# Routing a mixture of experts batch by batch inside the attention ahead of it, in a gated cross-attention stack

## The chip, the cores and the metric

The kernel runs on one core of a Trainium2 chip. The metric is the device time of one execution in microseconds (us). Three runs of the kernel before took 2361.58, 2368.78 and 2369.87 us; the median is 2368.78 us.

## The reference, cut to what matters

Eight batches of 256 rows with 256 features pass through four layers. Each layer adds a gated attention branch and then a gated feed-forward branch. The feed-forwards of layers 1 and 2 are mixtures of experts in which every row goes to 2 of 8 experts:

```python
x = x + tanh(g_xattn[1]) * L1_xattn(layernorm(x), ctx_768, mask, ...)     # stage l1x
x = x + tanh(g_ffn[1])   * L1_ffn(layernorm(x), ...)                      # stage l1f
x = x + tanh(g_xattn[2]) * L2_xattn(layernorm(x), ctx_768, ...)           # stage l2x
x = x + tanh(g_ffn[2])   * L2_ffn(layernorm(x), ...)                      # stage l2f
...
# L1_ffn: hidden width 682
gate_logits = x @ Wg.T ; top 2 of 8 ; gating = softmax over the two logits
out = sum over e of gating[e] * ((silu(x @ W1[e].T) * (x @ W2[e].T)) @ W3[e].T)
# L2_ffn: hidden width 256, and two shared experts that every row passes
scores = softmax(xt @ gate_w.T) ; top 2 of (scores + gate_bias) ; weights = scores of the two
out = sum over e of gate_e * expert_e(xt) + (silu(xt @ sw1.T) * (xt @ sw3.T)) @ sw2.T
```

## The kernel before

All 2048 rows stay in SBUF as `x`, 16 tiles of 128 rows, two tiles a batch (T = 2, B = 8, NT = 16, NE = 8 experts). Each engine runs its own list of instructions in the order in which it was written; engines wait for one another on semaphores. TensorE (PE) multiplies, VectorE (DVE), ScalarE (ACT) and GpSimd (POOL) do the rest, SyncE (SP) issues most DMAs. The stages run in the order l0x, l0f, l1x, l1f, l2x, l2f, l3x, sim, l3f; a semaphore `phase` counts the finished ones.

**Attention.** `packing` (l1x, l3x, l3f) runs over n = -3 .. B and inside over 16 heads h. While the heads of one batch are computed, the projections of batch n + 3 and the output of batch n - 1 are interleaved with them at fixed h; batch n - 1 is added to `x` on DVE at h = 8 (L1248). The scores that DVE takes maxima of (L1167) go round three PSUM banks in l1x and two in l3x; other results use "rooms", PSUM banks handed out in turn, two in l1x and three in l3x. `wide` (l2x) runs over i, 16 heads a batch, in the same way: POOL normalises each head's probabilities (L849, L852), PE transposes them three heads later, batch n is added to `x` at i = 16(n + 1) + 7 (L1096).

**Mixture.** `mixture` first chooses for all 16 tiles at once: DVE statistics (L923, L934), POOL the power -1/2 (L734), DVE the normal rows into `r.all` (L1326), PE transposes and logits (L2329, L2319), DVE the ranks of the 8 logits of a row (L1331 to L1357), PE the counts of rows ahead for each expert (L2339), DVE the slots and the numbers of the blocks and gates (L1370 to L1412). POOL then writes every row to its two places in the DRAM table `rows_by_expert` by 32 indirect DMAs (L807). SP reads the table back, 512 rows a job (L552), and the 15 jobs of experts begin. An expert's weights are split into a high and a low part on POOL (L793, L795) before PE multiplies (L1875 to L1877); l1f holds two sets of weights (ring 2), l2f five. In l2f four jobs on the shared experts stand ahead of the 15, but they too begin after the choice. The table is cleared once, by one DMA from ACT in l0f, and l2f uses it again.

## Time and profile before

| | |
|---|---|
| runs, us | 2361.58, 2368.78, 2369.87 |
| profiled execution, us | 2362.5 |
| its span, us | 2360.8 |
| PE, DVE, ACT, POOL busy | 81%, 58%, 34%, 33% |
| l1x ends, first product of the experts of l1f | 481.9 us, 584.4 us |
| l2x ends, first product of l2f | 1471.4 us, 1526.6 us |

The busy shares are means over stages. In l1x and l2x PE is busy nearly all the time; between the end of an attention and the first product of the experts it mostly waits.

### The profile page before, as it was taken

The numbers are of one execution on the slowest core, as the hardware profiler recorded it, in microseconds if no ns is written. First come the engines' busy times: TensorE is split into PE (matmuls) and PEld (weight loads), VectorE is DVE, ScalarE is ACT, GpSimd is POOL, SyncE is SP. The second block draws the span as 40 slices with busy tenths as digits, with TensorE's granted clock in tenths as the row PEclk, the third lists the DMA queues.
The fourth block names the chain that finished last, engine by engine and source line by source line (L and its number), as shares of the span: only waits on it lengthen the run. The fifth ranks groups of instructions, "written<-read, shape, count | busy, mean of one in ns | idle before, by whom it ended". The sixth has DMA issues, their size and how long they took to land.

```text
span 2360.8 us, 33280 instructions
## 1 busy us (share of the span) xinstructions
PE 1904.9 (81%) x11976; PEld 1489.9 (63%) x11976; DVE 1368.9 (58%) x2894; ACT 803.2 (34%) x1761; POOL 779.7 (33%) x694
## 2 busy tenths in 40 slices
PE   3579699941999999959999997599957888547997
PEld 2467566541777777747877776588855555335664
DVE  2434478551554444447677775565536898456774
ACT  1122146510222222136555553113312454123554
POOL 3110111055245444337666554635532200100000
PEclk9789779655999999979999999599975797777999
DMA  4280356213233333221111102025628542015341
GB/s 131 84 286 0 51 84 86 29 76 125 90 126 119 112 112 103 83 74 45 31 31 39 27 19 76 25 99 174 192 75 111 80 63 29 1 22 69 61 75 43
DMA packets 125310, 186.26 MB, mean 79 GB/s; under 512 B 11940, under 2 KB 106212, under 8 KB 122532
## 3 DMA queue, kind: packets, MB, share of 16 engines
q1 hardware_dynamic: 96212, 136.75, 25.5%
q0 software_dynamic: 8448, 26.52, 3.7%
q10 hardware_dynamic: 20496, 20.97, 2.7%
q8 instruction: 93, 1.52, 0.3%
q14 instruction: 61, 0.50, 0.1%
HBM read 89.26 MB, written 47.19 MB: 58 GB/s over the span
## 4 chain that ended last, share of the span: by engine, by line
PE 54%; issue 14%; DVE 13%; POOL 10%; DMA 5%; ACT 3%; SPq 1%; DVEq 0%; POOLq 0%; ACTq 0%
PE bank L1875 10%; PE bank L1876 8%; PE bank L1877 8%; PE bank L2156 6%; PE bank L2188 4%; POOL ewl L795 3%; DMA ew<-in_we 3%; PE bank L2008 2%; DVE nmf L1167 2%; PE bank L2025 2%; PE bank L2051 2%; PE bank L2173 1%; PE bank L2036 1%; POOL ewh L793 1%; POOL rows_by_expert L807 1%
## 5 line engine op out<-in xcount | busy, mean ns | idle before, releaser
L1167 DVE TENSOR_REDUCE nmf<-bank 128x2 f32<-128x512 f32 x384 | 260.3, 688 | 112.0 <-PE bank L2156 108.9
L1748 ACT ACTIVATE pT<-bank 128x512 f32<-128x512 f32 x384 | 224.8, 597 | 250.7 <-PE bank L2173 248.4
L1430 DVE TENSOR_TENSOR bank<-sil,bank 128x512 f32<-128x512 f32 x136 | 94.8, 697 | 283.1 <-ACT sil L1803 282.6
L2156 PE MATMUL bank<-kpack,qpack 48*128 48x256 f32 (+1 forms) x768 | 199.8, 367 | 52.4 <-DVE nmf L1167 28.5
L1875 PE MATMUL bank<-split,ewl 128*128 128x512 f32 x514 | 211.4, 411 | 24.0 <-POOL ewl L795 16.3
L1876 PE MATMUL bank<-split,ewh 128*128 128x512 f32 (+1 forms) x578 | 228.2, 395 | 0.0
L1877 PE MATMUL bank<-split,ewh 128*128 128x512 f32 (+1 forms) x578 | 227.3, 393 | 0.0
L2156 PEld LDWEIGHTS bank<-kpack,qpack 48*128 48x128 f32 (+1 forms) x768 | 127.4, 220 | 131.9 <-DVE nmf L1167 61.8
L795 POOL TENSOR_TENSOR ewl<-ew,ewh 128x1536 fp32r<-128x1536 f32 (+1 forms) x47 | 206.0, 4384 | 3.8
L2173 PE MATMUL bank<-qpack,kpack 50*128 50x256 f32 (+1 forms) x768 | 198.7, 360 | 9.5 <-ACT pT L1748 9.4
L793 POOL CAST ewh<-ew 128x1536 fp32r<-128x1536 f32 (+1 forms) x47 | 85.2, 1814 | 321.0 <-DMA ew<-in_we 310.1
L1803 ACT ACTIVATE sil<-bank 128x512 f32<-128x512 f32 x136 | 81.3, 598 | 320.0 <-PE bank L1877 320.0
L1649 ACT ACTIVATE w<-bank,nmax 128x256 f32<-128x256 f32 x256 | 118.9, 469 | 168.0 <-DVE nmax L1050 166.7
L1875 PE MATMUL bank<-ewh,split 128*128 128x256 f32 x544 | 167.2, 307 | 6.5 <-issue 6.5
L1876 PE MATMUL bank<-ewl,split 128*128 128x256 f32 x544 | 155.7, 286 | 0.0
L1877 PE MATMUL bank<-ewh,split 128*128 128x256 f32 x544 | 155.2, 285 | 0.0
L734 POOL TENSOR_TENSOR rstd<-rstd,mhalf 128x2 f32<-128x2 f32 x40 | 28.4, 711 | 376.5 <-DVE rstd L1151 247.3
L2173 PEld LDWEIGHTS bank<-qpack,kpack 50*128 50x128 f32 (+1 forms) x768 | 124.3, 213 | 25.9 <-ACT pT L1748 20.0
L1050 DVE TENSOR_REDUCE nmax<-bank 128x2 f32<-128x512 f32 x128 | 88.1, 689 | 87.6 <-PE bank L2025 86.1
L1875 PEld LDWEIGHTS bank<-split,ewl 128*128 128x128 f32 x514 | 97.6, 190 | 62.7 <-DVE split L1433 21.0
L852 POOL TENSOR_TENSOR w<-w,esum 128x512 f32<-128x512 f32 x128 | 133.2, 1040 | 10.1
L849 POOL TENSOR_TENSOR esum<-esum,minus 128x2 f32<-128x2 f32 x128 | 89.7, 701 | 139.1 <-ACT w L1649 138.8
(432 smaller groups left out, 4623.4 us busy)
## 6 DMA issues: line engine op xcount, KB each, us to landing
ew<-in_we SPq DMA_DIRECT2D x32, 768.0 KB, 7.6
ew<-in_we SPq DMA_DIRECT2D x15, 1408.0 KB, 6.2
rows_by_expert<-zeros ACTq DMA_DIRECT2D x1, 20480.0 KB, 62.9
kpack<-khl SPq DMA_DIRECT2D x144, 128.0 KB, 4.0
qpack<-qhl SPq DMA_DIRECT2D x144, 128.0 KB
arena<-rows_by_expert SPq DMA_DIRECT2D x23, 512.0 KB, 4.2
rows_by_expert<-arena SPq DMA_DIRECT2D x38, 256.0 KB, 5.3
split<-split SPq DMA_DIRECT2D x64, 128.0 KB, 2.5
```

The costliest lines, as they stand in the source:

```text
L793: nc.gpsimd.tensor_copy(high, whole).then_inc(m["wh"], 1)
L795: nc.gpsimd.tensor_tensor(low, whole, high, ALU.subtract).then_inc(m["ws"], 1)
L852: nc.gpsimd.tensor_tensor(p3, p3, total.rearrange("p (t o) -> p t o", o=1).broadcast_to([P, T, S]), ALU.mult).then_inc(m["pn"], 1)
L1167: V.tensor_reduce(nmf[:, c, :, j, r], bank[s.banks[i % len(s.banks)]][:, :] .rearrange("p (t k) -> p t k", t=T), AXX, ALU.max, negate=True ...
L1430: tt(whole, sil[n % 2][rr, :], whole, ALU.mult).then_inc(m["prod"], 1)
L1649: ins = A(probs[i % 4][:, t * S:(t + 1) * S], bank[i % 2][:, t * S:(t + 1) * S], ACT.Exp, bias=nmax[:, h, t:t + 1], accum_out=esum[:, h, t ...
L1748: A(pT16[i % 8][:, :], bank[2 + h % 2][:, :], ACT.Exp, scale=s.qscale).then_inc(m["e"], 1)
L1875: mm(out_, al, bh, start=start, stop=False)
L1876: mm(out_, ah, bl, start=False, stop=False)
L1877: return mm(out_, ah, bh, start=False, stop=stop)
L2156: ins = mm(bank[s.banks[i % len(s.banks)]][:, t * S:(t + 1) * S], q[rows, r, t * P:(t + 1) * P], k[rows, r, :], start=True, stop=True)
L2173: ins = mm(bank[2 + h % 2][:, t * S:(t + 1) * S], k[rows, r, t * P:(t + 1) * P], q[rows, r, :], start=True, stop=True)
```

## The change

Each batch is routed by itself, in the attention that ends with it, as soon as its rows are final. Statistics, normal rows, transposes, logits, ranks, running sums, slots and the writing of the rows (4 indirect DMAs a batch) are interleaved with the heads of the next two batches. `csum` carries how many rows each expert has so far, so that no batch needs the later ones. Part of the small arithmetic moves from DVE to POOL. l1x routes all eight batches (its loop gets two more rounds, in which only routing is left), l2x routes seven and the eighth is routed in l2f, beside the shared experts. Each mixture has a table of its own; the second is cleared by ten DMAs of 2 MB from ACT in jobs 2 to 11 of l1f. l1x now uses two banks for scores and three rooms. In l1f the first set of weights is split by ACT and DVE instead of POOL; the numbers of the blocks and the gates are worked out there ahead of the first job, in l2f within job 1.

```diff
-        self.banks, self.rooms = ((0, 1), (5, 6, 7)) if self.proj else ((0, 1, 5), (6, 7))
+        self.banks, self.rooms = (0, 1), (5, 6, 7)
+        self.last = B + 3 if mask else B + 1
...
@@ POOL, l1x @@
+                    if s is L1X and 0 <= n - 2 < B:
+                        route_rank(L1F, n - 2)
+                        route_sums(L1F, n - 2)
+                    if s is L1X and 0 <= n - 1 < B:
+                        route_root(L1F, n - 1)
...
+                        route_slots(L1F, n - 2, m[f"mf{b}"], at[f"mf{b}"] + k + 1)
+                        route_scatter(L1F, n - 2)
...
+            def route_rank(s, n):
+                pool.wait_ge(rt["cmp"], s.turn * B + n + 1)
+                tt(same, same, tri[:, :, :].rearrange("p (o e) j -> p o e j", o=1).broadcast_to([P, T, NE, NE]), ALU.mult)\
+                    .then_inc(rt["choice"], 1)
+                tt(more_, more_, same, ALU.add).then_inc(rt["choice"], 1)
+                tt(more_[:, :, :, 0:4], more_[:, :, :, 0:4], more_[:, :, :, 4:8], ALU.add).then_inc(rt["choice"], 1)
...
+            def route_scatter(s, n):
+                pool.wait_ge(rt["slot"], s.turn * B + n + 1)
+                for t in range(T):
+                    for w in range(2):
+                        nc.gpsimd.indirect_dma_start(
+                            tables[s.name].rearrange("b s d -> (b s) d"),
+                            bass.IndirectOffsetOnAxis(ap=sli[s.name][:, w, n * T + t:n * T + t + 1], axis=0),
+                            routed(n, t)[:, :], None).then_inc(mo[f"sc{n % 2}"], 16)
@@ POOL, mixture @@
-                root({"asked": asked[s.name]}, 1, rstda[:, :], rstda[:, :], mhalf[:, 0:NT])
-                pool.wait_ge(g["xn"], entered(s.name, B) * T)
-                for w in range(s.ring):
+                if s.shared:
+                    route_root(s, B - 1)
+                    split_set(0)
+                    route_rank(s, B - 1)
+                    split_set(1)
+                    route_sums(s, B - 1)
+                    route_slots(s, B - 1, rt["trc"], 1)
+                    route_scatter(s, B - 1)
+                else:
+                    pool.wait_ge(m["ws"], at["ws"] + s.parts)
+                for w in range(2 if s.shared else 1, s.ring):
                     split_set(w)
@@ POOL, l2x @@
+                    if i % 16 == 8 and 0 <= i // 16 - 1 < B - 1:
+                        route_root(L2F, i // 16 - 1)
+                    if i % 16 == 4 and 0 <= i // 16 - 2 < B - 1:
+                        route_rank(L2F, i // 16 - 2)
...
+                    if i % 16 == 12 and 0 <= i // 16 - 2 < B - 1:
+                        route_scatter(L2F, i // 16 - 2)
@@ DVE, l1x @@
+                        if s is L1X and h == 8 and 0 <= n - 1 < B:
+                            if n == B:
+                                free()
+                            route_stats(L1F, n - 1, ch)
+                        if s is L1X and h == 3 and 0 <= n - 2 < B:
...
+                            route_compare(L1F, n - 2)
+                        if s is L1X and h == 8 and 0 <= n - 2 < B:
+                            route_chosen(L1F, n - 2)
+                        if s is L1X and h == 14 and 0 <= n - 2 < B:
+                            route_places(L1F, n - 2, ch, *made("tr", n - 2))
+                        if s is L1X and h == 1 and 0 <= n - 3 < B:
+                            route_cast(L1F, n - 3)
@@ DVE, mixture @@
+                    for p in range(s.parts):
+                        dve.wait_ge(rt["high"], p + 1)
+                        whole, low, high = (weights(t, s, 0, p) for t in (ew, ewl, ewh))
+                        tt(low, whole, high, ALU.subtract).then_inc(m["ws"], 1)
...
+                if not s.shared:
+                    blocks_and_gates()
+                    low_part(0)
+                    low_part(1)
@@ PE @@
+            def route_turn(s, n, to, done):
+                pe.wait_ge(rt["rows"], s.turn * B + n + 1)
+                for t in range(T):
+                    for c in range(DC):
+                        ins = tr(to[:, c * S + t * P:c * S + (t + 1) * P], routed(n, t)[:, c * P:(c + 1) * P], ident[:, :])
+                ins.then_inc(done, 1)
+            def route_ranks(s, n, to, done):
+                pe.wait_ge(rt["pick"], s.turn * B + n + 1)
+                mm(to[:, 0:(T + 1) * NE], ones[:, :], csum[:, n * T:n * T + T + 1, :].rearrange("p t e -> p (t e)"),
+                   start=True, stop=False)
+                mm(to[:, 0:T * NE], strict[:, :], lg[:, n * T:n * T + T, :].rearrange("p t e -> p (t e)"), start=False, stop=True)\
+                    .then_inc(done, 1)
@@ ACT, l1f @@
+                    if not s.shared and 2 <= k < 12:
+                        act.dma_start(tables["l2f"][4 * k - 8:4 * k - 4, :, :].rearrange("b s d -> (b s) d")
+                                      .rearrange("(p k) d -> p k d", p=P), zeros[:, 0:1, :].broadcast_to([P, 16, D]))\
+                            .then_inc(g["zero2"], 16)
```

DVE where l1x ends and l1f begins, before (`x` is the last batch's sum, `lg` and `scr` hold logits and ranks of all tiles):

```order
L1248 SCALAR_TENSOR_TENSOR x<-both,tgx,x 128x512
L1318 MEMSET idle 128x1
L923 BN_STATS bsta<-x 128x6 x2
L932 MEMSET idle 128x1
L934 BN_AGGR mva<-bsta 128x2 x16
L936 TENSOR_SCALAR rstda<-mva 128x16
L1326 TENSOR_SCALAR arena<-x,mva,rstda 128x256 x16
L1331 COPY lg<-bank 128x128
L1332 TENSOR_REDUCE gm<-lg 128x16
L1333 TENSOR_TENSOR sel<-lg,gm 128x128
L1334 MEMSET idle 128x1
L1347 TENSOR_TENSOR scr<-lg 128x1024
```

The same place of the changed kernel (`sli_l1f` are the slots of one batch, `ewl` the low part of the first set of weights):

```order
L1428 SCALAR_TENSOR_TENSOR x<-both,tgx,x 128x512
...
L1106 TENSOR_TENSOR scr<-sel 128x128
L1107 TENSOR_TENSOR scr<-sel 128x128
L1113 TENSOR_SCALAR larger<-scr 128x16
L1114 TENSOR_SCALAR lg<-scr 128x16
L1118 COPY totals<-bank 128x8
L1119 TENSOR_TENSOR scr<-bank,ebase 128x16
L1125 CAST sli_l1f<-slf 128x2x2
L1557 TENSOR_TENSOR ewl<-ew,ewh 128x2816
L1557 TENSOR_TENSOR ewl<-ew,ewh 128x1536
L1558 TENSOR_REDUCE gm<-sel 128x16
L1559 TENSOR_TENSOR sel<-sel,gm 128x128
```

The sixteen normalised tiles and the operations over all tiles are gone from here; what is left is one batch's, and two subtractions of weights.

POOL in the middle of l2x, before (a head is one `esum` and one `w` row, L779 gathers rows of the mixture before):

```order
L734 TENSOR_TENSOR rstd<-rstd,mhalf 128x2
L779 DMA w<-rows_by_expert,sli 128x256 x4
L849 TENSOR_TENSOR esum<-esum,minus 128x2
L852 TENSOR_TENSOR w<-w,esum 128x512
L849 TENSOR_TENSOR esum<-esum,minus 128x2
L852 TENSOR_TENSOR w<-w,esum 128x512
```

The same place of the changed kernel:

```order
L750 TENSOR_TENSOR rstd<-rstd,mhalf 128x2
L870 DMA w<-rows_by_expert_l1f,sli_l1f 128x256 x4
L940 TENSOR_TENSOR esum<-esum,minus 128x2
L943 TENSOR_TENSOR w<-w,esum 128x512
L815 TENSOR_TENSOR scr<-scr,tri 128x128
L818 TENSOR_TENSOR scr<-scr 128x128
L820 TENSOR_TENSOR scr<-scr 128x16x4
L822 TENSOR_TENSOR scr<-scr 128x16x2
L824 TENSOR_TENSOR scr<-scr 128x16
L940 TENSOR_TENSOR esum<-esum,minus 128x2
L943 TENSOR_TENSOR w<-w,esum 128x512
```

Five additions for the ranks stand between two heads; nine more small operations and four indirect DMAs follow further down in the same batch.

## Rows read from the trace of the kernel before

**Rows 1.** Busy time by stretch: us, PE, PEld, DVE, ACT, POOL, PEclk, DMA share, GB/s.

```profile
340.00:360.00 20.00, 18.71 (x184) 12.70 (x180) 16.70 (x38) 12.55 (x24) 2.58 (x3) 1.00 0.70 93
...
440.00:460.00 20.00, 19.02 (x117) 10.65 (x106) 8.39 (x17) 8.91 (x18) 0.00 (x0) 0.50 0.01 2
...
482.00:530.00 48.00, 21.38 (x100) 20.73 (x100) 28.30 (x67) 5.09 (x9) 30.73 (x9) 0.50 0.24 93
530.00:583.00 53.00, 2.19 (x9) 1.83 (x10) 5.80 (x24) 1.09 (x2) 31.50 (x33) 0.50 0.36 124
...
1166.00:1218.00 52.00, 49.27 (x342) 41.17 (x341) 38.77 (x66) 29.89 (x92) 34.39 (x40) 0.97 0.14 35
```

**Rows 2.** Timeline between l1x and the experts of l1f: start, us, engine, operation, idle before.

```profile
481.15 0.75 DVE L1248 SCALAR_TENSOR_TENSOR x<-both,tgx,x 128x512 f32<-128x512 f32 x1
...
530.79 1.12 POOL L807 DMA_INDIRECT rows_by_expert<-arena,sli  x1 [10.13 <-DVE idle L1383]
...
570.19 0.96 POOL L807 DMA_INDIRECT rows_by_expert<-arena,sli  x1 [0.30 <-issue]
...
578.63 1.97 PE L2356 MATMUL bank<-ident,arena 128*128 128x128 f32 x8 [52.07 <-DMA arena<-rows_by_expert]
...
584.37 0.78 PE L1875 MATMUL bank<-split,ewl 128*128 128x512 f32 x1
```

**Rows 3.** Timeline between l2x and the products of l2f.

```profile
1470.60 0.75 DVE L1096 SCALAR_TENSOR_TENSOR x<-scr,tgx,x 128x512 f32<-128x512 f32 x1
...
1526.55 0.78 PE L1875 MATMUL bank<-split,ewl 128*128 128x512 f32 x1
```

**Rows 4.** Groups of POOL instructions over the span: shape, count, busy, mean ns, idle.

```profile
L795 POOL TENSOR_TENSOR ewl<-ew,ewh 128x1536 fp32r<-128x1536 f32 x32 | 112.7, 3522 | 2.6
L795 POOL TENSOR_TENSOR ewl<-ew,ewh 128x2816 fp32r<-128x2816 f32 x15 | 93.3, 6221 | 1.2
L849 POOL TENSOR_TENSOR esum<-esum,minus 128x2 f32<-128x2 f32 x128 | 89.7, 701 | 139.1 <-ACT w L1649 138.8
...
L807 POOL DMA_INDIRECT rows_by_expert<-arena,sli x64 | 61.8, 965 | 41.2 <-DVE idle L1383 22.3 <-issue 18.9
L793 POOL CAST ewh<-ew 128x1536 fp32r<-128x1536 f32 x32 | 47.2, 1474 | 87.9 <-DMA ew<-in_we 82.5 <-DVE arena L1326 5.4
L793 POOL CAST ewh<-ew 128x2816 fp32r<-128x2816 f32 x15 | 38.1, 2538 | 233.0 <-DMA ew<-in_we 227.7 <-DVE arena L1326 5.4
```

**Rows 5.** Timeline of the choice of l1f: DVE beside POOL, and the block numbers.

```profile
508.73 6.11 POOL L795 TENSOR_TENSOR ewl<-ew,ewh 128x2816 fp32r<-128x2816 f32 x1
508.76 6.22 DVE L1333 TENSOR_TENSOR sel<-lg,gm 128x128 f32<-128x128 f32 x1
...
529.82 0.17 DVE L1387 TENSOR_SCALAR more<-upto 128x8 f32<-128x8 f32 x1
...
534.94 0.29 DVE L1412 TENSOR_REDUCE gw_l1f<-scr 128x16 f32<-128x128 f32 x1
```

**Rows 6.** Timeline of PE: four transposes in l1x, four and logits in l1f.

```profile
361.74 0.66 PE L2107 MATMUL bank<-ident,xn 128*128 128x128 f32 x4
...
493.96 1.09 PE L2329 MATMUL bank<-ident,arena 128*128 128x128 f32 x4
...
494.84 1.71 PE L2319 MATMUL bank<-wg,xt 128*128 128x8 f32 x8
```

**Rows 7.** Waits, 1114 to 1426 us: waiting line, what it waited for, total, times, longest.

```profile
PE bank L2051 <- DVE sil L1057: 10.6, 5, 2.1
```

**Rows 8.** Waits, 584 to 1000 us.

```profile
PE bank L1875 <- POOL ewl L795: 16.3, 13, 2.7
```

**Rows 9.** The page's DMA queues and issues: packets, MB, share; KB each, us to landing.

```profile
q10 hardware_dynamic: 20496, 20.97, 2.7%
...
ew<-in_we SPq DMA_DIRECT2D x15, 1408.0 KB, 6.2
rows_by_expert<-zeros ACTq DMA_DIRECT2D x1, 20480.0 KB, 62.9
```

More of the change, by code:

```diff
@@ L79, in jobs @@
             jobs.append(("x", (i + 9) // 16))
+        for what, at, back in (("tx", 11, 1), ("tl", 15, 1), ("tr", 7, 2)):
+            if i % 16 == at and 0 <= i // 16 - back < B - 1:
+                jobs.append((what, i // 16 - back))
         return jobs
@@ L471, in build @@
         asked, requests = {}, 0
-        for n, one in (("l0x", 1 + B), ("l0f", 1 + B), ("l1x", B), ("l1f", 1), ("l2x", B), ("l2f", 1), ("l3x", B),
+        for n, one in (("l0x", 1 + B), ("l0f", 1 + B), ("l1x", B), ("l2x", B), ("l3x", B),
                        ("sim", 2), ("l3f", B)):
@@ L480, in entries @@
         def entries(name, n):
-            return n + sum(B for k in n_phase if n_phase[k] < n_phase[name] and k not in packs and k != L2X.name)
+            return n + sum(B for k in n_phase if n_phase[k] < n_phase[name] and k in ("l0x", "l0f", "sim"))
         def entered(name, n):
-            return n + (n_phase[name] - 1) * B
+            return n + sum(B for k in n_phase if n_phase[k] < n_phase[name] and k not in ("l1f", "l2f"))
         @block.sync
@@ L757, in packing @@
                     gather(L2F, 2)
[L758 removed]
+                for n in range(-3, B + 2 if s is L1X else B):
                     p = n + 3
@@ L1264, in finish, with free @@
                                 ALU.mult, ALU.add))
+                def free():
+                    for b, rooms_ in enumerate(s.rooms):
+                        last = max(k for (what, n), (r, k) in s.place.items() if r == b and what[0] != "t")
+                        dve.wait_ge(m[f"mf{b}"], at[f"mf{b}"] + last + 1)
+                    V.memset(idle[:, 0:1], 0.0).then_inc(g["phase"], 1)
                 def clipped(i):
@@ L1274, in packing @@
                 normal(0)
-                for n in range(-3, B + 1):
+                if s is L1X:
+                    ch.link(V.memset(csum[:, 0, :], 0.0))
+                for n in range(-3, s.last):
                     for h in range(NH):
@@ L1294, in packing @@
                             register_maxima(n + 2)
-                        if n == B and h < B - 1 and not s.own:
+                        if n == B and h < B - 1 and s is L3X:
                             stats_of(h)
@@ L1314, in packing @@
                     finish(B - 1)
-                for b in range(2):
-                    dve.wait_ge(m[f"mf{b}"], at[f"mf{b}"] + s.used[b])
+                if s is not L1X:
+                    free()
                 s.total["dve"] = ch.k
-                V.memset(idle[:, 0:1], 0.0).then_inc(g["phase"], 1)
                 return at["dve"] + ch.k
@@ L1374, in mixture @@
-                ch.link(tt(before, before, bank[1][:, NT * NE:2 * NT * NE].rearrange("p (e t) -> p e t", e=NE), ALU.add))
-                ch.link(tt(part[2], before.rearrange("p e t -> p t e"), ebase[:, 0:1, :].broadcast_to(full), ALU.add))
-                for w in range(2):
-                    ins = tt(part[w], part[2], both[w][:, :, :], ALU.mult)
-                ch.link(ins)
-                for w in range(2):
-                    ins = V.tensor_reduce(slf[:, w, :], part[w], AXX, ALU.add)
@@ L1381, in mixture @@
-                ch.link(ins)
-                ch.link(V.tensor_copy(sli[:, :, :], slf[:, :, :]))
-                V.memset(idle[:, 0:1], 0.0).then_inc(m["sl"], 1)
-                extra, start, end, value = (more[:, k, :] for k in range(4))
-                rows_of = upto[:, :, NT - 1]
-                ch.link(ts(extra, rows_of, 512.0, None, ALU.is_gt))
-                ch.link(stt(extra, rows_of, 1024.0, extra, ALU.is_gt, ALU.add))
-                ch.link(stt(extra, rows_of, 1536.0, extra, ALU.is_gt, ALU.add))
@@ L1741, in gathered, with route_copy, route_rows @@
                     copy(oT16[:, 2 * f:2 * f + 2, :], halves(bank[4])).then_inc(m["oc"], 1)
+                def route_copy(n):
+                    if n > 0:
+                        made("tl", n - 1)
+                    from_, done = made("tx", n)
+                    copy(xt[:, :, :], halves(from_)).then_inc(done, 1)
+                def route_rows(n):
+                    act.wait_ge(rt["root"], 3 * n + 3)
+                    act.wait_ge(mo[f"sc{n % 2}"], L1F.base[f"sc{n % 2}"] + 64 * (n // 2))
+                    for t in range(T):
+                        r = n * T + t
+                        ins = A(routed(n, t)[:, :], x[:, r, :], ACT.Identity, scale=rstda[:, r:r + 1], bias=shift[:, t:t + 1])
+                    ins.then_inc(rt["rows"], 1)
                 def exponent(n, h):
@@ L1755, in packing @@
                     copy(masks[:, :, :], halves(from_[0:16, :])).then_inc(done, 1)
-                for n in range(-3, B + 1):
+                for n in range(-3, s.last):
                     for h in range(NH):
@@ L2269, in packing @@
                     ins.then_inc(done, 1)
-                for n in range(-3, B + 1):
+                for n in range(-3, s.last):
                     for h in range(NH):
```

448 lines of the change are left out of this document (297 added, 151 removed).

## The prediction

> **What bounds the kernel now.** I read the busy time by stretch first. In l1x, PE is busy 18.71 of 20 us at a granted clock of 1.00 (2.4 GHz), DVE 16.70; in l2x PE 49.27 of 52, POOL 34.39; but between 482 and 583 us PE works 23.6 of 101 us, at 0.50 (1.2 GHz) [rows 1]. The timelines give that hole its edges. From the end of the last sum of l1x (481.15 + 0.75 = 481.9) to the first product of l1f (584.37) pass 102.5 us; from the last sum of l2x (1471.35) to the first product of l2f (1526.55) pass 55.2 us [rows 2, 3]. Within the first hole, 40 us go to the 32 indirect writes, which POOL starts 1.265 us apart (570.19 - 530.79, divided by 31), and 13.2 us from the end of the last write (571.15) to the product: landing, reading back, transposing, splitting [rows 2]. The holes sum to 157.7 us. The attentions that are to take this work in have little room: PE about 6% in both, and DVE 17% in l1x.
>
> **The choice of l1f.** What can't be streamed is the last batch. I follow its chain from 481.9. Prices: DVE as at 529.82 to 535.23, some 0.2 to 0.3 us an operation [rows 5]; POOL's subtractions of 1536 and 2816 columns take 3.52 and 6.22 us, so 2.11 ns a column and 0.28 us fixed, which I extend down to 0.3 to 0.55 us for the small ones; a power on two columns takes 0.70 [rows 4]. In order: statistics 1.4; DVE marks the experts of batch 6, 0.4; POOL's sums for it and the three operations on the last batch's root, 2.2; POOL's slots of batch 6, 1.6, and DVE's cast, 0.2; the four writes of batch 6, 5.1 (the last batch's rows, transposes 1.1, logits 1.7 and comparison lie beside these [rows 6]); then the last batch: ranks 2.2, marks 0.4, sums 0.6, counts on PE 1.0, places 0.5, slots 1.6, cast 0.3, writes 5.1. Together 22.6, and about 1.0 for some fifteen handovers: the last write ends at 505.5, not 571.15.
>
> With the same 13.2 us behind it the first product would come at 518.7. But DVE must first finish the block numbers and gates, which now precede `low_part(0)`, and POOL splits the second set of weights at that very time: 2.54 + 6.22 + 1.47 + 3.52 = 13.8 us, from 505.5 to 519.3 [rows 4]. In the trace a DVE operation on two SBUF tensors that began 0.03 us behind POOL's 6.11 us subtraction took 6.22 us, where its like take 0.3 [rows 5]. So I let DVE pass one such operation for each of POOL's four, leave about 5 of its 5.4 + 1.6 us of work until after 519.3, and add the 3.0 us that low part, transposes and first product took: first product at 527.3, a gain of 57 us. Bounds: 68 if DVE isn't held and the small POOL operations take 0.3; 48 if every one takes 0.70 and DVE gets nothing done before POOL ends.
>
> **The choice of l2f.** Seven batches are routed when l2x ends, but the seventh's cast and four writes still stand before POOL's root of the eighth: 1.6 statistics, 1.0 places, 1.6 slots, 5.1 writes, 0.7 root. The eighth batch's rows then go through 0.7 rows, 1.1 transposes, 0.6 copy, 1.1 high, 0.7 low, 2.0 transposes, 1.0 logits: the first product comes 17 us after l2x ends, not 55.2, a gain of 38. Part is given back. Sum over the first shared job: PE needs the second set before its third tile and also waits for the running sums, which POOL reaches only after ranks (from 22 us) and a split of 5.0: 7 us of stall. Then in job 1 DVE's 7 us of numbers meet POOL's splits of sets 2 to 4 (15 us), and PE, which has two tiles in store, waits about 6. I take 38 - 13 = 25; bounds 38 and 12.
>
> **What l1x pays.** PE gains per batch four transposes 0.66, logits about 0.9 (8 records, half of the 1.71 at the low clock) and counts 0.5: 2.1 us at the full clock, 3.8 at the low one [rows 6]. It has 1.3 us of idle a batch [rows 1]. DVE gains 2.8 us on 16.7, POOL about 10 us on 2.6. Two banks instead of three for the scores bring DVE's maxima closer to PE; the third room takes away about as many waits, so I set the exchange at nothing (its cover is DVE's remaining slack; if that is gone it costs another 1 us a batch). Three batches at the full clock by 2.3, the first one 1, and the last three at the low clock, where PE has 1 us idle in 20 [rows 1], by 3.1: 17 us. Bounds: 6 if the idle time takes it in, 32 if DVE becomes the bound.
>
> **What l2x pays.** Per batch PE gets 2.1 us of work. Its waits there are for DVE, 2.1 us once a batch, at the heads where the former mixture is added in [rows 7]; the logits and keys of the routed batch (1.6 us of DVE) fall on the same heads and make that wait longer. POOL gets ranks 2.2, sums 0.9, root 0.7, slots 1.6 and writes 5.1, 10.5 on 34.4 of 52; the writes come in one piece between two heads 2.6 us apart, of which POOL needs 1.8, so PE sees about 1 of the 5.1 us behind a store of three heads. Less what overlaps: 4.3 us a batch, seven batches, 30 us. Bounds 10 and 60.
>
> **The clearing of the second table.** The one clearing moved 20480 KB in 62.9 us [rows 9]; a tenth is 6.3 us of all DMA engines, issued in ten jobs of l1f, 0.6 us behind the load of the next weights, which lands in 6.2 us. Behind that load stand a cast 2.54 and a subtraction 6.22, and PE already waits 1.25 us a job for them (16.3 over 13) [rows 8], so each us of delay is paid in full. The zeros travel as 20496 packets of 1 KB [rows 9], a row of weights has 11 KB. If the DMA engines take a packet from each in turn, the load lasts 1/11 longer, 0.6 us; ten jobs pay 7 us. That is my value; bounds 0 and 63 (the two share the bytes evenly until the zeros are through).
>
> The Trainium skill, in DMA: Bandwidth & Descriptors, section Queues, rings and completion order, says that each DMA engine goes round its queues packet by packet; by it the price is the 7 us. The same passage calls packets of 9 to 17 descriptors typical; if the zeros went so, their turns would be as long as those of the weights, and the price would be nearer the 63. The trace of before never has both under way at once, so no row decides.
>
> **The sum.** 2362.5 for the profiled execution (span 2360.8 and 1.7 around it) - 57 - 25 + 17 + 30 + 7 = 2334.5. The median of the runs lies 6.3 above that execution, the lowest run 0.9 below; I add 2: 2336 us.
>
> **The rivals.** *Routing is nearly free in the attentions.* For it: PE's idle 6% and its third room; against: both PE and DVE are near full in l1x. With both at their lower bounds, 11 + 20 less: 2305.
>
> *l2x pays twice that.* If the small POOL operations cost 0.70 like the power [rows 4], fourteen of them and the writes make 14.9, POOL is busy 49.3 of 52 before any gap between instructions, and every burst reaches PE. 8.6 us a batch: 2336 + 30 = 2366. Against: the straight line through POOL's subtractions.
>
> *The clearing holds up the weights.* Place: the end of each of jobs 2 to 11 of l1f; price 6.3 us each, 63 in place of 7: 2392, slower than before. It decides from about 4 us a job on (2336 + 33 reaches the median). For it: both transfers start together and either alone fills the engines; against: the size of the packets.
>
> *The clock of l1x.* Before, it is 0.50 as soon as the projections end, although PE is busy 19.02 of 20 us [rows 1]. If two banks and the new waits thin PE's work while the projections still run, four transposes cost 1.09 instead of 0.66 [rows 6], a full batch some 12 us more, six batches 72: 2408.
>
> **How the numbers follow.** Forecast 0.54 (its own range 2310 to 2360), free routing 0.17, dear l2x 0.12, clearing 0.12, clock 0.05. About 0.5%, 12 us, is what a measurement of this kernel can tell from no change: faster means under 2357, slower over 2381. Faster: 0.52 of the forecast's 0.54, all 0.17, 0.03 of dear l2x, 0.01 of the clearing: 0.73. Same: 0.02 + 0.07 + 0.03 = 0.12. Slower: 0.02 + 0.08 + 0.05 = 0.15. For 8 in 10 the range takes in free routing down to 2292 and the clearing up to 2392.
>
> **What would show it.** Right: POOL's last write of l1f ends near 505 plus what l1x grew (about 17), and PE's first product some 22 us later; one DVE operation of several us in front of it; l2f's first product about 17 us after l2x's last sum, then a stall of some 7 us. A batch of l1x near 22.5 us at the full clock and of l2x near 56. PE's wait for `ewl` in l1f about 2 us a job. Wrong: a batch of l1x at or over 24 us or at a clock of 0.5 before the projections end; waits of PE for POOL's `w` in l2x of several us a batch; a load of weights landing after 10 us or more; or the first product of l1f later than 70 us after the last sum, which would mean that the chain of the last batch is longer than I counted.

## The result and the profile after

| | before | changed |
|---|---|---|
| runs, us | 2361.58 to 2374.60 (4) | 2419.65 to 2425.63 (4) |
| median, us | 2369.32 | 2422.92 |
| profiled span, us | 2360.8 | 2421.8 |

The changed kernel takes 1.0228 times as long, 95% interval 1.0197 to 1.0260: slower beyond doubt, though whether by more than 2% stays unclear. It was forecast at 2336 us, faster. The stages, from the first and last rows of each in the two traces:

| stretch | before | changed | difference | forecast |
|---|---|---|---|---|
| start to end of l1x | 481.9 | 544.3 | +62.4 | +17 |
| to the first product of l1f | 102.5 | 44.4 | -58.0 | -57 |
| to the first sum of l2x | 546.4 | 580.1 | +33.7 | +7 |
| first to last sum of l2x | 339.8 | 375.1 | +35.3 | +30 |
| to the first product of l2f | 55.2 | 20.9 | -34.3 | -38 |
| to the first gathered row added in l3x | 228.2 | 247.2 | +19.0 | +13 |
| the rest | 606.1 | 608.9 | +2.8 | 0 |

The two holes closed nearly as forecast, 92.3 us together. What was given back is 150.4 us instead of 67. Half of that gap is in l1x. The changed kernel by stretch (columns as in [rows 1]):

```profile
340.00:430.00 90.00, 82.84 (x580) 54.99 (x579) 55.89 (x143) 41.95 (x82) 21.44 (x46) 0.71 0.45 67
...
782.00:1057.00 275.00, 240.34 (x1215) 196.66 (x1213) 107.72 (x157) 45.50 (x78) 98.70 (x31) 0.91 0.40 133
...
1169.00:1545.00 376.00, 341.43 (x2344) 283.62 (x2344) 276.71 (x528) 192.03 (x583) 255.76 (x353) 0.96 0.15 44
```

The kernel before, for the same work:

```profile
340.00:430.00 90.00, 83.76 (x798) 55.38 (x794) 73.65 (x163) 55.93 (x107) 7.74 (x9) 1.00 0.71 92
...
777.00:1020.00 243.00, 223.33 (x1195) 183.69 (x1194) 106.17 (x154) 45.61 (x78) 96.82 (x30) 0.98 0.30 98
1131.00:1471.00 340.00, 318.56 (x2232) 263.99 (x2232) 241.63 (x402) 187.31 (x569) 204.50 (x235) 0.99 0.14 39
```

Read the first row of each together. PE is busy nearly as much of the 90 us (82.84 against 83.76), but the trace has 580 records of products instead of 798: the granted clock is 0.71 instead of 1.00. Busy time alone would have shown nothing. The clock is lower in the second half of l1f (0.91 against 0.98) and in l2x too.

The hole before l1f, answering [rows 2]:

```profile
543.56 0.75 DVE L1428 SCALAR_TENSOR_TENSOR x<-both,tgx,x 128x512 f32<-128x512 f32 x1
...
567.44 0.96 POOL L859 DMA_INDIRECT rows_by_expert_l1f<-others,sli_l1f  x1 [0.31 <-issue]
...
571.03 6.11 POOL L886 TENSOR_TENSOR ewl<-ew,ewh 128x2816 fp32r<-128x2816 f32 x1
```

DVE beside it, answering [rows 5], and PE:

```profile
571.07 6.16 DVE L1579 TENSOR_TENSOR scr<-more,ebase 128x64 f32<-128x64 f32 x1
...
585.71 1.29 DVE L1534 TENSOR_TENSOR split<-bank,split 128x512 fp32r<-128x512 f32 x2
...
588.74 0.78 PE L2113 MATMUL bank<-split,ewl 128*128 128x512 f32 x1
```

The last write ends 24.1 us after l1x (forecast 23.6). Then DVE's 6.16 us on 64 columns, whose like take 0.22, is one of four operations that pass one by one with POOL's (the others take 3.31, 1.37 and 2.90 us).

The hole before l2f, answering [rows 3]. The two normal rows that take 0.7 us elsewhere take 5.02, beside POOL's split:

```profile
1543.96 0.75 DVE L1262 SCALAR_TENSOR_TENSOR x<-scr,tgx,x 128x512 f32<-128x512 f32 x1
...
1553.56 5.02 DVE L1079 TENSOR_SCALAR others<-x,mva,rstda 128x256 f32<-128x256 f32 x2 [1.30 <-POOL rstda L803]
...
1565.65 0.77 PE L2113 MATMUL bank<-split,ewl 128*128 128x512 f32 x1
```

PE's waits in l1f, 589 to 1057 us, and in l2f, 1565 to 1640 us, answering [rows 8]:

```profile
PE bank L2113 <- POOL ewl L886: 34.2, 13, 4.6
```

```profile
PE bank L2113 <- DVE split L1612: 9.5, 3, 9.0
PE bank L2144 <- POOL csum L832: 3.9, 1, 3.9
```

DMA, answering [rows 9]: the weights land in 7.5 us instead of 6.2, the zeros in 15.9 us for 2 MB.

```profile
q10 hardware_dynamic: 41136, 41.94, 5.2%
...
ew<-in_we SPq DMA_DIRECT2D x15, 1408.0 KB, 7.5
...
rows_by_expert_l2f<-zeros ACTq DMA_DIRECT2D x10, 2048.0 KB, 15.9
```

### The profile page after: what moved, and what is told of

It reads as the page before. It is cut to its first block, busy times and chain, and to the rows that moved or that the text cites. A ratio compares the mean times of both kernels' runs of the same rounds, so it can differ in the third digit from the quotient of the medians.

```text
span 2421.8 us, 33847 instructions
## 1 busy us (share of the span) xinstructions
PE 1971.2 (81%) x12032; PEld 1530.3 (63%) x12032; DVE 1402.9 (58%) x3014; ACT 815.7 (34%) x1794; POOL 832.0 (34%) x926
## 4 chain that ended last, share of the span: by engine, by line
PE 51%; DVE 15%; issue 14%; POOL 10%; DMA 5%; ACT 3%; SPq 1%; DVEq 0%; POOLq 0%; ACTq 0%
PE bank L2113 10%; PE bank L2114 8%; PE bank L2115 8%; PE bank L2424 6%; PE bank L2456 4%; DMA ew<-in_we 4%; POOL ewl L886 3%; DVE nmf L1347 3%; PE bank L2269 2%; PE bank L2312 2%; POOL ewh L884 1%; PE bank L2286 1%; POOL w L870 1%; PE bank L2297 1%; PE bank L2466 1%
## 5 line engine op out<-in xcount | busy, mean ns | idle before, releaser
L2424 PE MATMUL bank<-kpack,qpack 48*128 48x256 f32 (+1 forms) x768 | 217.8, 390 | 63.8 <-DVE nmf L1347 44.1
L2113 PE MATMUL bank<-split,ewl 128*128 128x512 f32 x514 | 219.8, 428 | 50.9 <-POOL ewl L886 34.2
L2114 PE MATMUL bank<-split,ewh 128*128 128x512 f32 (+1 forms) x578 | 235.5, 407 | 0.0
L2115 PE MATMUL bank<-split,ewh 128*128 128x512 f32 (+1 forms) x578 | 234.6, 406 | 0.0
L2424 PEld LDWEIGHTS bank<-kpack,qpack 48*128 48x128 f32 (+1 forms) x768 | 137.7, 235 | 151.6 <-DVE nmf L1347 81.2
L2441 PE MATMUL bank<-qpack,kpack 50*128 50x256 f32 (+1 forms) x768 | 208.5, 372 | 5.3 <-ACT pT L1968 5.1
L886 POOL TENSOR_TENSOR ewl<-ew,ewh 128x1536 fp32r<-128x1536 f32 (+1 forms) x45 | 195.0, 4333 | 3.6
L2441 PEld LDWEIGHTS bank<-qpack,kpack 50*128 50x128 f32 (+1 forms) x768 | 131.3, 222 | 14.9 <-ACT pT L1968 12.8
L2115 PEld LDWEIGHTS bank<-split,ewh 128*128 128x128 f32 (+1 forms) x578 | 114.0, 197 | 26.2
## 6 DMA issues: line engine op xcount, KB each, us to landing
rows_by_expert_l2f<-zeros ACTq DMA_DIRECT2D x10, 2048.0 KB, 15.9
```

The costliest lines, as they stand in the source:

```text
L886: nc.gpsimd.tensor_tensor(low, whole, high, ALU.subtract).then_inc(m["ws"], 1)
L2113: mm(out_, al, bh, start=start, stop=False)
L2114: mm(out_, ah, bl, start=False, stop=False)
L2115: return mm(out_, ah, bh, start=False, stop=stop)
L2424: ins = mm(bank[s.banks[i % len(s.banks)]][:, t * S:(t + 1) * S], q[rows, r, t * P:(t + 1) * P], k[rows, r, :], start=True, stop=True)
L2441: ins = mm(bank[2 + h % 2][:, t * S:(t + 1) * S], k[rows, r, t * P:(t + 1) * P], q[rows, r, :], start=True, stop=True)
```

## The experiments

Eighteen kernels ran, on four chips: e1 to e4 on one, e5 to e8 and e13 to e16 on another, e9 to e12 on a third, e17 and e18 on the last. The kernel before ran beside each group: its median was 2395 us with e1 to e4, 2391 with e17 and e18, and 2369 to 2370 with all others. Only ratios are compared over groups. The table also gives stretches of each kernel's trace (us; clock: granted, 340 to 430 us; end: end of the last sum of l1x; l1f: first product to the first sum of l2x; l2f: first product to the first gathered row added in l3x). Each is of one execution: with the same code for a stage, l1f takes 545.2 to 557.4 us in the kernels built on before, and the end of l1x moves from 530.1 to 538.5 us between e16 and e17. A difference of a few us in one stretch shows nothing by itself.

| kernel | clock | l1x end | l1f | l2f | ratio to before, 95% |
|---|---|---|---|---|---|
| before | 1.00 | 481.9 | 546.4 | 228.2 | |
| changed | 0.71 | 544.3 | 580.1 | 247.2 | 1.0197 to 1.0260 |
| e1 before, two banks | 1.00 | 491.2 | 545.2 | 253.6 | 1.0016 to 1.0056 |
| e2 changed, three banks | 0.68 | 555.2 | 575.5 | 247.9 | 1.0128 to 1.0209 |
| e3 clearing early in l0f | | 571.7 | 552.9 | 247.6 | 1.0074 to 1.0155 |
| e4 e2 and e3 | | 583.4 | 546.1 | 247.2 | 1.0123 to 1.0210 |
| e5 clearing late in l0f | 0.70 | 545.7 | 545.4 | 247.3 | 1.0083 to 1.0170 |
| e6 e5, dense product a head | 0.98 | 549.5 | 545.5 | 247.2 | 1.0087 to 1.0168 |
| e7 before, small work | 0.75 | 541.7 | 555.6 | 228.9 | 1.0186 to 1.0287 |
| e8 before, dense tail | 1.00 | 477.6 | 546.7 | 228.3 | 0.9947 to 0.9992 |
| e9 before, transposes | 1.00 | 474.1 | 545.7 | 228.4 | 0.9944 to 1.0018 |
| e10 before, 8 products | 0.78 | 528.0 | 545.9 | 228.3 | 1.0131 to 1.0276 |
| e11 before, dense in rooms | 1.00 | 482.0 | 557.4 | 229.0 | 0.9987 to 1.0045 |
| e12 e8, and l3x | 1.00 | 481.7 | 547.3 | 227.9 | 0.9988 to 1.0043 |
| e13 before, 4 products | 0.90 | 504.8 | 547.0 | 228.4 | 1.0059 to 1.0193 |
| e14 e5, wide logits | 0.80 | 533.2 | 550.6 | 247.1 | 1.0053 to 1.0114 |
| e15 e14 in l2x too | 0.80 | 530.4 | 551.0 | 247.9 | 1.0062 to 1.0128 |
| e16 e14 and e8 | 0.80 | 530.1 | 545.5 | 247.2 | 1.0024 to 1.0064 |
| e17 e16, numbers late | 0.80 | 538.5 | 567.2 | 243.4 | 0.9973 to 1.0024 |
| e18 e17, dense from batch 2 | 0.99 | 539.1 | 568.9 | 243.6 | 0.9981 to 1.0039 |

In e3 and e4 l1x begins some 34 us later, so their clock in this window is left out.

The ratios of e1 to e4 need care. The trace of e1, built on before, has 25 us more in l2f; e2 to e4, built on the changed kernel, do not. If the kernel before lost its 26 us on that chip in the same place, which no trace shows, the ratios of e2 to e4 come out about 1% too low: e3's median, 2423.04 us, is that of the changed kernel, 2422.92. e17 and e18 may profit in the same way.

**e1 and e2: the banks.**

```
e1, in before:       self.banks, self.rooms = (0, 1), (5, 6, 7)
e2, in the changed:  ... ((0, 1), (5, 6, 7)) if self.proj else ((0, 1, 5), (6, 7))
```

> The kernel before, with l1x alone on two banks for scores and three rooms; nothing is routed in the attention. Banks theory (two banks let DVE's maxima stop PE, and these stops alone keep the granted clock at 0.5 for much of l1x): l1x ends 40 us later or more, mean clock between 320 and 430 us under 0.8, time near 2410 us. Routing theory (it is the routed batches' work and waits that thin PE's stream): l1x within 5 us of before, clock 1.00 between 320 and 430, time 2365 to 2375 us.

> The changed kernel, with l1x back on three banks for scores and two rooms. Banks theory: the clock returns to 1.00 while the projections run, l1x ends near 500 us instead of 544, time 2375 to 2385 us. Routing theory: l1x as in the changed kernel, clock about 0.67, time 2415 to 2430 us, or more, as five results per batch share two rooms.

The banks theory fell. Two banks alone cost 9.3 us, nearly all before the first sum (351.7 against 343.0), and the clock then stays at 1.00; three banks with two rooms make the changed kernel's l1x 11 us longer. Something in the routed work takes the clock.

The 9.3 us go with a lower clock too, ahead of the window of the table. Before, e1 and the changed kernel, from 321 to 341 us:

```profile
321.00:341.00 20.00, 19.49 (x188) 13.18 (x184) 16.09 (x37) 12.90 (x25) 2.58 (x3) 1.00 0.52 83
```

```profile
321.00:341.00 20.00, 19.45 (x120) 12.47 (x114) 10.56 (x26) 8.06 (x16) 1.30 (x2) 0.53 0.45 53
```

```profile
321.00:341.00 20.00, 20.00 (x121) 12.74 (x122) 10.41 (x24) 7.84 (x15) 2.58 (x3) 0.50 0.45 68
```

The clock rises to 1.00 about 20 us later than before, and the first sum comes 8.7 us later in e1 and 10.2 in the changed kernel.

**e3, e4, e5: the clearing.** The ten DMAs go; the second table is cleared by one:

```
e3, ACT:  act.dma_start(tables["l1f"]..., zeros...); act.dma_start(tables["l2f"]..., zeros...)
e5, SP:   sp.wait_ge(g["zero"], 16); sp.dma_start(tables["l2f"]..., zeros...)
```

> The changed kernel, with the second table cleared by one DMA behind that of the first in l0f, and none in l1f. Clearing theory (the zeros hold up the weights of jobs 2 to 11, and the waits pull the clock down): l1f shorter by about 30 us, weights land in 6 us again, PE waits 16 us for ewl instead of 34, time near 2392 us. Rival (POOL and DVE, not the zeros, made l1f longer): under 8 us gained, 2415 us or more. The 63 us of zeros in l0f stand beside little other traffic and should cost nothing there.

> The changed kernel with both edits: three banks and two rooms in l1x, and the second table cleared in l0f. If both causes hold and add up: 2423 - 42 - 31 = 2350 us, under the kernel before (2369). If only the clearing holds, 2392; if only the banks hold, 2380.

> The changed kernel, with the second table cleared by one DMA that SyncE issues once the first clearing has landed (about 167 us), in the middle of l0f; none in l1f. The clearing in l0f by ACT behind the first one took 34 us there because its issue held ACT for 56.7 us. Theory: nothing is issued while the queue is full, l0f is as before, l1f gains the 27 us that its shortening showed, time 2392 to 2398 us (against 2423). Rival: 20 MB of zeros beside l0f slow it by themselves: l1x starts 10 us or more later and the time stays at 2405 or above.

e3 shortened l1f by 27 us and gave it all back in l0f: the first sum of l1x comes 32 us later. ACT stood in the issue of the second DMA until the first one's zeros were nearly through (timeline of ACT and its queue, e3):

```profile
104.94 0.65 ACTq L2086 DMA_DIRECT2D rows_by_expert_l1f<-zeros  x1
...
105.63 56.72 ACTq L2088 DMA_DIRECT2D rows_by_expert_l2f<-zeros  x1
...
162.46 0.60 ACT L1758 ACTIVATE xt<-bank 128x512 f32<-128x512 f32 x1 [55.96 <-issue]
```

In e5, issued at 169.08 behind a wait for the first clearing, it costs l0f next to nothing (first sum of l1x 354.5 against 353.2). l1f takes 545.4 us, as before the change, and PE waits 16.5 us for the weights where the changed kernel has 34.2:

```profile
783.00:1024.00 241.00, 222.34 (x1198) 182.50 (x1197) 106.64 (x155) 45.60 (x78) 97.05 (x31) 0.99 0.30 99
```

```profile
PE bank L2112 <- POOL ewl L889: 16.5, 13, 2.4
```

So in this pair of traces the ten clearings cost 34.7 us: 18 as waits for the weights, the other 17 as longer busy time of PE, where the clock falls to 0.91 (second half of l1f: 240.34 us for 1215 records against 222.34 for 1198). The medians give back less, 22 us (2422.92 against 2400.58): the rest of e5's trace, behind l2f, is 10 us longer than the changed kernel's, for no edit there. e4 was to add two gains of which neither came; 2430.53 us.

**e6: buying the clock back.** One line ahead of the scores of each head:

```
if s is L1X: mm(bank[...][:, :], wqs16[:, 0, 0, 0:P], wqs16[:, 0, :, :], start=True, stop=True)
```

> The former kernel, and in l1x one product of 128 rows by 512 columns ahead of the scores of each head, into the bank that the scores then overwrite: it waits for nothing, and its result is used by nobody. It adds 128 x 0.23 = 29 us of PE's work at the full clock, 55 at the low one. Density theory (the routed work is transposes and products of 8 to 24 columns, and these thin PE's stream until the clock falls): the clock rises to 1.00 in l1x, and the stage takes no longer than without, 175 to 190 us, in spite of the added work. Wait theory (the clock falls at PE's waits for the routed rows, which stay): mean clock stays near 0.67, l1x takes 225 us or more.

The clock came back to 0.98 between 340 and 430 us with all waits in place, but the stage ends 4 us later and the median is that of e5 (2399.45 against 2400.58): 29 us of added work ate the gain, and from 430 to 550 us the clock is 0.74.

**e7, e9, e10, e11, e13: what takes the clock.** All on the kernel before, in the rooms of the maxima, where only PE gets more to do:

```
e9:   4 x tr(to[:, t*P:(t+1)*P], ident, ident)
e10:  8 x mm(to[:, 0:8], ident, ident[:, 0:8]); mm(to[:, 0:24], ones, ...); mm(to[:, 0:16], strict, ...)
e7:   e9 and e10
e13:  e10 with 4 x instead of 8 x
e11:  in each of two rooms 5 x mm(to[:, 0:512], wqs16[...128 columns], wqs16[...512 columns])
```

> The kernel before, with PE's part of the routing alone added in l1x, in the rooms of the maxima: per batch four transposes, eight products of 8 columns, two of 24 and 16, on constants. No engine but PE has more to do and nothing new is waited for. Density theory: the clock falls below 1.00 while the projections run, as in the changed kernel, and l1x ends 35 us later or more. Wait theory: the clock stays at 1.00 up to 430 us and l1x ends 8 x 2.1 = 17 us later or less.

> The kernel before with four more transposes a batch in l1x, on constants, and no small products: one half of what cost 60 us in l1x. If the transposes drive the clock down: mean clock between 340 and 430 us under 0.9, l1x ends 30 us later or more, time over 2395 us. If the products of few columns do it: clock 1.00 up to 430, l1x ends 5 to 8 us later (8 x 0.66), time 2370 to 2380.

> The other half: the kernel before with eight products of 8 columns and two of 24 and 16 a batch in l1x, and no more transposes. If the products of few columns drive the clock down: clock about 0.7 between 340 and 430 us, l1x ends 40 us later or more, time over 2405 us. If it is only the amount of added work, each half alone costs about half of the 60 us.

> The control for both: the kernel before with ten products of 128 rows by 512 columns a batch in l1x, in the same rooms and at the same heads as the added small work, 2.3 us a batch at the full clock (the small work took about as long). Density theory: the clock stays at 1.00 and may last beyond 430 us; l1x ends 18 us later at most. Rival (any work added to a full PE costs the clock, whatever its shape): clock under 0.8, l1x ends 40 us later or more.

> The kernel before with PE's few-column work in the number that the routing has: per batch of l1x four products of 8 columns and two of 24 and 16, on constants. Width theory: these are enough; the clock is under 0.9 between 340 and 430 us and l1x ends 30 us later or more (the changed kernel: 62, with everything else of the routing). Rival: it took the double number; with the right one the clock stays at 1.00 and l1x ends under 15 us later, so that the changed kernel lost its clock through waits as well.

One error of mine stands in the first expectations: the trace writes two records for each product in full precision, so its 8 rows for the logits are four products. e7 and e10 had twice the routing's number; e13 has the right one. Windows of e7, e13 and e11:

```profile
340.00:430.00 90.00, 87.41 (x637) 61.41 (x634) 54.50 (x126) 39.99 (x76) 7.72 (x9) 0.75 0.42 63
```

```profile
340.00:430.00 90.00, 84.85 (x729) 58.25 (x728) 63.46 (x144) 48.24 (x93) 9.60 (x11) 0.90 0.57 79
```

```profile
340.00:430.00 90.00, 88.03 (x788) 59.52 (x788) 68.27 (x152) 51.97 (x99) 9.35 (x11) 1.00 0.56 81
430.00:480.00 50.00, 42.45 (x364) 25.39 (x364) 28.22 (x63) 26.65 (x51) 0.00 (x0) 0.91 0.20 23
```

In e7 PE is busy 97% of the window, more than before, and the clock is 0.75: this loss needs no waits. In e10 the clock falls between 341 and 351 us, while PE never stands still (its columns as in [rows 1]):

```profile
331.00:341.00 10.00, 9.28 (x86) 6.62 (x88) 8.98 (x24) 6.48 (x13) 0.70 (x1) 1.00 0.38 69
341.00:351.00 10.00, 10.00 (x61) 8.05 (x50) 2.88 (x5) 2.55 (x7) 1.09 (x2) 0.59 0.17 28
```

Transposes do not cause it: in e9 the clock stays at 1.00, and l1x even ends 8 us earlier, since from 430 to 480 us it is 0.73 instead of 0.53 (the interval of its ratio takes in 1). As many microseconds of wide products do not either: e11 adds ten of them a batch, the clock stays up beyond 430 us, and l1x ends where it did. The small products cause it: l1x ends 46 us later with eight and two a batch, 23 us with four and two. e13 lies between its two theories, 0.90 and 23 us where one asked for 30 or more and the other for under 15. And 13.8 of its 23 us come before the first sum, where the clock rises late as in e1 (0.50 from 321 to 341 us); after it a batch takes 21.6 us instead of 20.3, and one takes 26.1.

These five kernels leave one rival: the small products also differ in format from the wide ones (full precision, two records each, against one), and e9's transposes stand at another place in the batch. Only e14, next, changes the number of columns alone. The Trainium skill (TensorE: Matmul & The Clock Gate, section HAM oscillation) explains a clock that keeps falling by waits of PE for data. That agrees with l1f, where waits and a lower clock came together (34.2 us, 0.91), but not with e7.

**e14, e15, e16: the changed kernel with wide logits.**

```
mm(to[:, t*NE:(t+32)*NE] as 32 x 8, xt[...], wg[:, c:c+1, :].broadcast_to([P, 32, NE]), ...)
mm(to[:, 0:240] as 10 x 24, ones, csum[...].broadcast_to([P, 10, 24]), ...)
```

> The changed kernel with the clearing in the middle of l0f (e5, 2400 us), and in l1x the logits' four products run over 32 copies of the 8 columns, the first of the two for the counts over 10 copies of its 24: 256 and 240 columns instead of 8 and 24. Every wait is as it was; PE has about 1.5 us a batch more to do. Width theory: the clock returns to 1.00 for most of l1x while the projections run, l1x ends 30 to 45 us earlier than in e5 (545), time 2355 to 2370. Wait theory: clock 0.67 as before, l1x ends 10 to 20 us later, time 2410 or more.

> As e14, and the same in l2x and l2f. l2x has a clock of 0.96 where it had 0.99; its four dips per 375 us are worth about 8 us, the wide products cost 7 x 1.5 = 10 us of PE, which waits for DVE once a batch anyway. Width theory: between 8 us faster and 5 us slower than e14. If the dips come from the waits there (PE stands 3 us at a time for DVE and POOL): 5 to 10 us slower than e14.

> As e14, with the product of 128 x 512 ahead of the scores of batches 5 to 7 in l1x, which brought the kernel before 7 us. The tail of l1x is longer here (the last two batches are routed in it). Forecast: 5 to 12 us faster than e14, near 2352 us, under the kernel before (2369). Rival: the tail waits for the routing chain of the last batches, not for PE: no gain on e14.

With nothing changed but the width, l1x ends 12.5 us earlier than in e5, the median is 12.9 us lower (2387.65 against 2400.58), and the clock goes from 0.70 to 0.80, although these products take 10.6 us instead of 4.0 in three batches:

```profile
L2138 PE MATMUL bank<-wg,xt 128*128 128x8 f32 x24 | 4.0, 294 | 2.7 <-ACT xt L1758 2.7
```

```profile
L2138 PE MATMUL bank<-wg,xt 128*128 128x256 f32 x24 | 10.6, 623 | 2.7 <-ACT xt L1761 2.7
```

The first fence is of the changed kernel, the second of e14, both 353 to 448 us. The gain is a third of what the expectation named: width is one cause of the low clock in the changed kernel, not the only one. In l2x width does nothing but cost: the clock stays at 0.96, and e15 takes 383.2 us from first to last sum, against 375.7. The dense tail raises the clock from 430 to 480 us to 1.00 from 0.81 and gives 7.5 us in the medians (e16), but l1x ends only 3 us earlier than in e14 and where it does in e15, which has no such tail.

**e8 and e12: wide products in the kernel before.**

```
e8:   if s is L1X and n >= 5: mm(the product of e6)
e12:  if s is L1X and n >= 5 or s is L3X: mm(the same)
```

> The kernel before, with the product of 128 x 512 ahead of the scores of the heads of batches 5 to 7 in l1x (48 of them), where the projections end and the clock falls to 0.5. Density theory: the clock stays at 1.00 for most of the stretch from 430 to 482 us; 48 x 0.23 = 11 us are added and up to 25 given back: l1x ends 5 to 15 us earlier than before. Wait theory, or a clock that no such filling holds: the clock is 0.5 from 430 us, l1x ends 15 to 20 us later.

> The kernel before with the product of 128 x 512 ahead of the scores in the last three batches of l1x, as in the run that gained 7 us, and in all batches of l3x, where the granted clock swings between 0.5 and 1.0. Density theory: l3x stays nearer 1.00; since DVE is busy over 18 of 20 us there, it can end 0 to 15 us earlier: time 2350 to 2363. Rival: PE's added 29 us are paid in full: 2375 to 2390.

e8 is the one kernel whose interval lies below the kernel before: 2362.98 us, ratio 0.9969 (0.9947 to 0.9992), a gain of 0.3%. The clock from 430 to 480 us is 0.87 instead of 0.53, for 48 more products, and l1x ends 4.3 us earlier, a little less than the 5 to 15 expected. Windows of e8, and of the kernel before:

```profile
430.00:480.00 50.00, 41.45 (x340) 22.05 (x329) 29.58 (x79) 24.86 (x48) 0.13 (x1) 0.87 0.11 16
```

```profile
430.00:480.00 50.00, 44.47 (x270) 24.59 (x270) 20.89 (x49) 21.08 (x41) 0.00 (x0) 0.53 0.01 2
```

In l3x the same product costs more than it gives: in e12 the clock is higher (0.82 against 0.76 over the stage), but from the first gathered row added to the last sum pass 285.5 us instead of 273.1.

**e17 and e18: DVE behind POOL.**

```
-                    blocks_and_gates()          # l1f: ahead of low_part(0)
-                        if s.shared and (k, i) == (1, 1):
+                        if (k, i) == ((3, 1) if s.shared else (1, 1)):
                             blocks_and_gates()
```

> As e16, and the block numbers and gates are worked out later, at times when POOL splits no weights: in l1f within job 1 instead of ahead of the first low part, in l2f within job 3 instead of job 1. Theory (DVE's small operations stand behind POOL's subtractions, and PE behind DVE): l1f's first product comes 9 us earlier after l1x's end than the 45 us of the changed kernel, and the 9 us wait of PE in job 1 of l2f goes with the dip of the clock behind it, 9 to 14 us: together 2380 - 20 = 2360 us, under the kernel before (2369). Rival (something else is late there next, such as the rows read back or POOL's splits themselves): under 8 us gained, 2372 or more.

> As e17, with the product of 128 x 512 ahead of the scores from batch 2 of l1x on instead of batch 5: 11 us more of work where the clock is about 0.8. Density theory: the clock comes to 1.00 there, 12 us given back against 11 paid: within 4 us of e17. Rival (the waits for DVE and for the routed rows hold the clock down between 380 and 440 us): 8 us slower than e17.

The hole before l1f shrank from 45.7 to 36.6 us, 9.1 as expected, and l2f by 3.8 of the 9 to 14. But l1f grew by 22: in job 1 the numbers met POOL's split of the next weights, which I had taken to come later. Waits of PE in e17, 575 to 1050 us, and the timeline of DVE and POOL:

```profile
PE bank L2111 <- DVE split L1615: 26.0, 31, 18.2
```

```profile
613.37 2.50 DVE L1570 SCALAR_TENSOR_TENSOR more<-totals,more 128x8 f32<-128x8 f32 x1
...
615.93 6.16 POOL L889 TENSOR_TENSOR ewl<-ew,ewh 128x2816 fp32r<-128x2816 f32 x1
616.42 5.71 DVE L1577 TENSOR_TENSOR more<-more 128x8 f32<-128x8 f32 x1
...
622.16 1.38 DVE L1578 TENSOR_TENSOR more<-ebase,more 128x8 f32<-128x8 f32 x1
...
623.83 3.32 DVE L1580 TENSOR_TENSOR scr<-more,ebase 128x64 f32<-128x64 f32 x1
```

An operation on 8 columns takes 5.71 us, until POOL's subtraction ends. The Trainium skill (SBUF — State Buffer, section SBUF: two separate sides) states that DVE with two SBUF inputs and GpSimd hold a common port for a whole instruction and the other waits; this trace agrees. e17 ends level with the kernel before by its ratio (0.9998), but on a chip where that kernel took 22 us more than on the other two; e17's own median is 9 us above e16's, and its l1f lost more (22 us) than the hole before it and l2f gained (9.1 and 3.8). So e17 is not shown to be better than e16. e18 has a clock of 0.99 between 340 and 430 us and still ends l1x where e17 does: its added products cost what the clock gives.

## Why the prediction was wrong

**l1x, +17 forecast, +62.4 measured: the step that failed.** I priced PE's added work by time, "2.1 us at the full clock, 3.8 at the low one", and assumed that three batches would run at the full clock as before. PE's idle time, by which I judged the cover, hardly moved between 340 and 430 us (7.2 us against 6.2). The rival on the clock named what came, a lower clock while the projections run, and got 0.05, because I tied it to two banks and to waits; its price was too high (72 us on top of the 17, measured 45). l1x from first to last sum, before, changed and e13:

```profile
343.00:481.90 138.90, 125.52 (x1040) 77.81 (x1032) 93.48 (x207) 75.43 (x145) 7.74 (x9) 0.83 0.44 57
```

```profile
353.20:544.30 191.10, 169.02 (x1148) 109.19 (x1140) 102.53 (x266) 86.39 (x173) 60.81 (x137) 0.67 0.34 58
```

```profile
356.80:504.80 148.00, 133.63 (x1112) 87.41 (x1104) 93.16 (x207) 75.53 (x145) 7.73 (x9) 0.85 0.37 51
```

Of the 62.4 us, 10.2 come before the first sum and 52.2 after it; of the 52.2, PE's busy time takes 43.5, where the prediction had 2.1 to 3.8 us a batch, and its idle time 8.7. From sum to sum the first four batches take 31.9, 34.4, 29.9 and 30.9 us instead of 20.3: the prediction's own sign of being wrong, "a batch of l1x at or over 24 us". The causes can't be added up from the single runs, since e1 and e13 each lose their time mostly before the first sum (8.7 of 9.3, 13.8 of 22.9). After it e1 gives the banks 0.6 us and e13 gives the small products 9.1; e14, with wide ones, takes 10 us back. So some 40 of the 52.2 us are not separated: e14 still runs at 0.80 with the routing's waits in place, and e6 and e18 show that the clock can be had back but not for nothing. This part stays open.

**The clearing, +7 forecast, +33.7 measured.** Shown by e5, which gives 34.7 back in l1f and 22 in the medians. The value came from a turn-by-turn sharing of packets; the even sharing would have made 63. By the rule of the Trainium skill (DMA: Bandwidth & Descriptors, section Queues, rings and completion order), taken packet by packet of 1 KB, it is 7, and with the long packets that it calls typical nearer 63; the measured value lies between the two. How the DMA engines share between the two streams I did not measure. The sum also had no term for the clock, though in the second half of l1f it is 0.91 beside the zeros and 0.99 without (e5).

**l2x, +30 forecast, +35.3 measured.** Right within its bounds. PE's idle time grows by 13 us (34.6 of 376 against 21.4 of 340), its busy time by 23, of which 15 were the forecast work; the other 8 I put down to the clock, 0.96 against 0.99. What lowers it there no run shows; wide products leave it at 0.96 (e15).

**l1f's hole, -57 forecast, -58.0 measured**, with the last write and the four operations held behind POOL where they were put. e17 confirms the term: moved away, they free 9.1 us. (The writes are 1.271 us apart by the two rows, not 1.265; the 40 us stand.)

**l2f, -38 + 13 forecast, -34.3 + 19.0 measured.** The first product comes 20.9 us after l2x, not 17, because the rows of the last batch stand 5 us behind a split. The waits in l2f are the two foreseen, 3.9 us for the running sums and 9.0 in job 1, where I had 7 and 6: the sum of 13 is right by luck; 6 more I have not traced to one row, but the clock is 0.63 between 1609 and 1621 us, behind the wait of 9.0.

The terms were added as if the rivals excluded each other. Two of them, the clock of l1x (45 of 72 us) and the clearing (27 of 56), came about half true together, and no case of mine held that.

## What to carry to other kernels

Before small products are pushed into a stage where TensorE runs at the full clock, price the clock and not only their microseconds: compare the granted clock and the number of products in equal windows, since the share of busy time hardly changes. Small DVE arithmetic that moves must be laid against the other engine's long operations at its new place, not only at the old one. A transfer that "nobody waits for" is free only where no load that somebody waits for runs beside it; 20 MB of zeros cost 35 us in l1f by the trace (22 by the medians) and about 1 us in the middle of l0f.

## What the runs showed of the hardware

- With four products of 8 columns and two of 16 and 24 a batch, all in full precision, the granted clock between 340 and 430 us was 0.90 where it had been 1.00 (e13), with eight and two 0.78 (e10), while PE was busy 94 and 97% of the window. With ten products of 512 columns a batch it stayed at 1.00, and between 430 and 480 us it was 0.91 instead of 0.53 (e11).
- The issue of a second DMA of 20480 KB on a queue where one is under way held ACT for 56.72 us; ten of 2048 KB did not.
- In e1 ACT stood three times, 31.4 us in all, beside POOL's indirect writes in l2f, for no releaser on this core that the trace shows; l2f took 25 us longer than in any other kernel built on before. The kernel before was 26 us slower on that chip. I have no trace of it there, so that the two are one is only likely.

```profile
1562.86 0.60 ACT L1803 ACTIVATE sil<-bank 128x512 f32<-128x512 f32 x1 [17.65 <-remote]
1572.77 0.60 ACT L1803 ACTIVATE sil<-bank 128x512 f32<-128x512 f32 x1 [9.31 <-remote]
```
